# A merged router and expert product, a reordered second phase and a reordered end in a 16-batch transformer kernel

## The reference

```python
x = x + ln(attention(ln(x)))       # 16 heads of 8, softmax over 512 keys
x = x + ln(fp8_ffn(ln(x)))         # 128 x 128 product on values rounded to fp8
x = x + ln(hawk_block(ln(x)))      # below
x = x + ln(moe(ln(x)))             # below

# hawk_block: z = rmsnorm(x) @ W_in; gate, xc = z; xc = causal conv of 4 taps
alpha = exp(-8 * softplus(base) * sigmoid(forget))   # forget, inp = xc @ W_gates
h = linear_recurrence(alpha, sqrt(1 - alpha**2 + 1e-6) * sigmoid(inp) * xc)
x = x + (gelu(gate) * h) @ W_out
x = x + (gelu(xn2 @ W_grow_a) * (xn2 @ W_grow_b)) @ W_shrink   # xn2 = rmsnorm(x)

# moe: 8 experts with one shared weight, capacity 100 tokens for each expert
logits = hs @ w_gate; gate = max(softmax(logits)); best = argmax(logits)
place = running count of the tokens that chose the same expert, over all batches
out = gate * (place < 100) * (hs @ w_expert + b_expert)
```

## Time and profile before

| what | value |
|---|---|
| runs | 1344.32 us median, 1343.93 to 1347.55 |
| the profiled execution | 1344.07 us, of which the span is 1342.4 us |
| PE busy | 1200.6 us (89%) |
| DVE busy | 1117.4 us (83%) |
| ACT busy | 974.6 us (73%) |
| POOL busy | 806.7 us (60%) |
| chain that ended last | PE 36%, DVE 25%, issue 15%, POOL 10%, ACT 10% |

### The profile page before, as it was taken

One profiled execution on the slowest core, in us unless ns is written; L12 is line 12 of the kernel. 1 busy time (PEld: TensorE's weight loads), 2 busy tenths in 40 slices (PEclk: granted clock), 3 DMA queues, 4 the chain that ended last, 5 costly groups with the idle time before them and its releaser, 6 DMA issues.

```text
span 1342.4 us, 26167 instructions
## 1 busy us (share of the span) xinstructions
PE 1200.6 (89%) x8688; PEld 498.3 (37%) x8688; DVE 1117.4 (83%) x2357; ACT 974.6 (73%) x1780; POOL 806.7 (60%) x1091
## 2 busy tenths in 40 slices
PE   1789999999999999999999999988989999999863
PEld 0223233332333333333333332334645555555443
DVE  2877999999999999999999899956668878878756
ACT  1267877888788788878788777787776787787640
POOL 6304447466466566566565545366788888788752
PEclk7589999999999999999999999999999999999985
DMA  1121011011011010110110010000000000000000
GB/s 50 52 89 43 27 45 40 30 43 40 30 44 38 31 43 32 37 44 33 37 45 31 32 37 15 2 1 1 1 9 9 9 17 9 9 16 9 16 9 24
DMA packets 52517, 37.87 MB, mean 28 GB/s; under 512 B 8864, under 2 KB 51744, under 8 KB 52384
## 3 DMA queue, kind: packets, MB, share of 16 engines
q1 hardware_dynamic: 52384, 36.22, 8.4%
HBM read 6.31 MB, written 4.19 MB: 8 GB/s over the span
## 4 chain that ended last, share of the span: by engine, by line
PE 36%; DVE 25%; issue 15%; POOL 10%; ACT 10%; SPq 4%; DMA 0%; ACTq 0%; DVEq 0%; POOLq 0%
PE bank L201 10%; PE bank L182 9%; DVE neg_max L493 9%; PE bank_pair L169 4%; PE bank L228 4%; SPq L644 3%; PE bank L210 3%; ACT probs L381 2%; PE bank L235 2%; DVE probs L1178 2%; PE bank_pair L797 2%; DVE probs L1350 2%; DVE probs L1354 1%; DVE y_q L472 1%; POOL x_all L1497 1%
## 5 line engine op out<-in xcount | busy, mean ns | idle before, releaser
L381 ACT ACTIVATE probs<-bank 128x512 f32<-128x512 f32 x1024 | 569.3, 599 | 166.1 <-PE bank L182 163.8
L493 DVE TENSOR_REDUCE neg_max<-bank_pair 128x2 f32<-128x1024 f32 x512 | 610.3, 1215 | 87.4 <-PE bank_pair L169 85.5
L182 PE MATMUL bank<-q_stack,k_stack 50*128 50x512 bf16 x1024 | 353.1, 388 | 29.9 <-ACT probs L381 22.7
L201 PE MATMUL bank<-probs,v_pad 128*32 128x256 f32 x4096 | 332.2, 394 | 0.4 <-issue 0.2
L169 PE MATMUL bank_pair<-k_stack,q_stack 48*128 48x512 bf16 x1024 | 292.4, 396 | 34.0 <-DMA k_stack<-k_parts 18.1
L182 PEld LDWEIGHTS bank<-q_stack,k_stack 50*128 50x128 bf16 x1024 | 79.7, 94 | 273.8 <-ACT probs L381 233.2
L201 PEld LDWEIGHTS bank<-probs,v_pad 128*32 128x32 f32 x4096 | 83.1, 108 | 167.5 <-issue 160.3
L797 PE MATMUL bank_pair<-probs,w_gates 128*128 128x512 f32 x256 | 118.9, 609 | 1.7 <-issue 1.7
L567 POOL TENSOR_SCALAR tiny<-mv_b 128x4 f32<-128x4 f32 x16 | 3.6, 228 | 147.6 <-DVE mv_b L52 147.6
L522 POOL TENSOR_TENSOR q_rest<-q_rest,q_parts 128x512 f32<-128x512 f32 x16 | 20.2, 1261 | 119.3 <-ACT q_rest L325 119.3
L169 PEld LDWEIGHTS bank_pair<-k_stack,q_stack 48*128 48x128 bf16 x1024 | 54.1, 95 | 59.5 <-DVE neg_max L493 37.3
(11 more groups left out here) (249 smaller groups left out, 2263.6 us busy)
## 6 DMA issues: line engine op xcount, KB each, us to landing
q_stack<-q_parts SPq DMA_DIRECT2D x384, 32.0 KB
k_stack<-k_parts SPq DMA_DIRECT2D x384, 32.0 KB
x_all<-in_z_dram SPq DMA_DIRECT2D x16, 256.0 KB, 3.0
out_dram<-x_all SPq DMA_DIRECT2D x16, 256.0 KB, 2.3
q_stack<-max_rows SPq DMA_DIRECT2D x64, 8.0 KB
w_gates<-in_w_gates_dram SPq DMA_DIRECT2D x1, 512.0 KB, 3.6
w_in<-in_w_in_dram SPq DMA_DIRECT2D x1, 256.0 KB, 2.7
w_grow<-in_w_grow_dram SPq DMA_DIRECT2D x1, 256.0 KB, 3.9
```

The costliest lines, as they stand in the source:

```text
L182: nc.tensor.matmul(st_ps[h][:, :], k_stack[par][rows, p, c * P:(c + 1) * P], q_stack[par][rows, p, :], start=True, stop=True).then_inc(s[" ...
L201: mm = nc.tensor.matmul(acc[32 * g:32 * g + 32, cols], v_pad[bpar][:, kc, 4 * a + g, :], probs[:, at + g, cols], start=(t == 0 and kc == 0 ...
L381: nc.scalar.activation(probs[:, 4 * (n % RING) + g, :], st_ps[g % 2][:, :], ACT.Exp, scale=SCALE)\
L493: nc.vector.tensor_reduce(neg_max[j // 4][:, c, j % 4, :], score_ps[c % 2][:, :, :], AX_X, ALU.max, negate=True).then_inc(s["max_read"], 1)
```

## The change

It does five things, all in the second phase.

1. **Joined product.** The router's weight (128x8) and the expert's (128x128) lie side by side in one tile `w_route_expert` of 136 columns; the logits and the expert product of a chunk come out of one matmul. The result no longer fits one bank, so the last two single banks become a pair: chunks 0 and 1 lie in its first half, chunks 2 and 3 in its second, each 136 columns wide, and the running counts move to column 384 of the second half. `shrink`, which writes the first half, now also waits until the logits have been read (`top_step`).
2. **Order in the loop.** ACT does `decay` ahead of `route_exps`. DVE does `ranks` after `stats_t` instead of ahead of `sum_h`. POOL does `root_x3` ahead of `roots_ahead`.
3. **Order at the start of the drain.** PE does `gate_in` ahead of `cumulated`; ACT does `decay` ahead of `route_exps`.
4. **Order at the end.** POOL: `root_x3(NB+2)` ahead of the routing roots of NB+1. DVE: `norm_x3(NB+2)` ahead of `ranks(NB+2)`; `routed_out(NB+1)` moves from ahead of `raw_x3(NB+2)` to behind `place(NB+2)`. Batch 14 uses the tile `acc_y` and statistics tiles of its own instead of y, so that it needs not wait for y. For the last batch the maximum and the shifted logits come ahead of the sum with the bias, and the statistics' aggregation behind the reciprocal.
5. **Dropped.** The last batch's counts (two small DVE instructions).

```diff
 def routed(i, free=None):                                   # tensor
-                for c in range(C):
-                    mm = nc.tensor.matmul(log_ps[:, c * E:(c + 1) * E], h4T[:, c * P:(c + 1) * P], w["route"][:, :],
-                                          start=True, stop=True)
-                mm.then_inc(s["logits_ps"], 1)
...
                 for c in range(C):
-                    mm = nc.tensor.matmul(bank_y[:, c * D:(c + 1) * D], h4T[:, c * P:(c + 1) * P], w["expert"][:, :],
+                    mm = nc.tensor.matmul(both_ps[:, c // 2, c % 2, :], h4T[:, c * P:(c + 1) * P], w["route_expert"][:, :],
                                           start=True, stop=True)
                 mm.then_inc(s["y_ps"], 1)
-        def shrink(i, free=None):
+        def shrink(i, free=None, after_logits=0):
...
                 if free:
                     wait(pe, *free)
+                    if after_logits:
+                        wait(pe, s["top_step"], 2 * after_logits)
                 else:
                     bank_free(pe, i, live, BANK_Y, "shrink")
+                    if live(i, -4):
+                        wait(pe, s["top_step"], 2 * (i - 3))
...
 PE, drain
             forget(NB)
+            gate_in(NB)
             cumulated(NB)
-            gate_in(NB)
 ACT, loop and drain
+            decay(i)
             route_exps(i)
-            decay(i)
 DVE
+        def y_of(i):
+            return (acc_y, "y_odd") if i == NB + 2 else (y, "y")
+        def largest(i):
+            b, q = i - 4, s["top_step"]
+            wait(dve, s["y_ps"], b + 1)
+            nc.vector.tensor_reduce(top[:, 0, :].rearrange("p (n c) -> p n c", n=2), log_ps, AX_X, ALU.max)\
+                .then_inc(q, 1)
+        def below_largest(i):
...
         def routed(i):
...
+                if i > NB + 2:
+                    largest(i)
+                    below_largest(i)
                 if i > NB + 1:
-                    wait(dve, s["x4_ready"], b)
+                    wait(dve, s["x4_ready"], b - 1)
                 else:
                     wait(dve, s["yc_ready"], b)
...
 DVE, drain
             norm_t(NB + 2)
-            routed_out(NB + 1)
             raw_x3(NB + 2)
             stats_x3(NB + 2)
             routed(NB + 2)
+            norm_x3(NB + 2)
             ranks(NB + 2)
             exps_sum(NB + 2)
             exps_inv(NB + 2)
-            norm_x3(NB + 2)
             counts_of(NB + 2)
             place(NB + 2)
+            routed_out(NB + 1)
             place_sum(NB + 2)
...
-            counts_of(NB + 3)
+            stats_y(NB + 3)
 DVE, loop
             routed(i)
-            ranks(i)
             sum_h(i)
             sum_t(i)
             stats_t(i)
+            ranks(i)
 POOL, loop
             x3_sum(i)
+            root_x3(i)
             roots_ahead(i)
-            root_x3(i)
 POOL, drain
             x3_sum(NB + 2)
+            root_x3(NB + 2)
             routed_root(NB + 1)
             routed_sum(NB + 1)
-            root_x3(NB + 2)
```

More of the change, by code:

```diff
@@ L708, in hawk_moe_phase @@
     xc_pad = padded[:, 0:T + TAPS - 1]
-    stats = {n: (sb(f"bn_{n}", [P, C, 6]), sb(f"mv_{n}", [P, C, 2])) for n in ("t", "x3", "y")}
+    stats = {n: (sb(f"bn_{n}", [P, C, 6]), sb(f"mv_{n}", [P, C, 2])) for n in ("t", "x3", "y", "y_odd")}
     h_sum = sb("h_sum", [P, C])
@@ L909, in cumulated @@
                 for c in range(C - 1):
-                    later = bank_r[:, 2 * C * E + (c + 1) * E:3 * C * E]
+                    later = bank_r[:, CUM + (c + 1) * E:CUM + C * E]
                     nc.tensor.matmul(later, consts["ones"][:, :],
@@ L969, in tensor @@
             routed(NB + 1, (s["t_ready"], NB - 1))
-            shrink(NB + 2, (s["y_ready"], NB - 2))
+            shrink(NB + 2, (s["y_ready"], NB - 2), after_logits=NB - 2)
             cumulated(NB + 1)
@@ L1119, in scalar @@
         if drain:
+            decay(NB)
             route_exps(NB)
-            decay(NB)
             square(NB)
@@ L1191, in taps, with stats_y @@
                     conv[par][:, 1, :], ALU.mult, ALU.add).then_inc(q, 1)
+        def y_of(i):
[6 more added lines that the diff above has]
+        def below_largest(i):
+            b, q = i - 4, s["top_step"]
+            wait(dve, q, 2 * b + 1)
+            wait(dve, s["route_step"], 5 * b)
+            wait(dve, s["exps_ready"], b)
+            TT(by_bank(shifted[:, :, :]), log_ps,
+               by_bank(top[:, 0, :].unsqueeze(2)).to_broadcast([P, 2, 2, E]), ALU.subtract).then_inc(q, 1)
+        def stats_y(i):
+            if live(i, -4):
+                aggregate(y_of(i)[1], "y", i - 4)
         def routed(i):
@@ L1195, in routed @@
                 b = i - 4
+                y, which = y_of(i)
                 wait(dve, s["y_ps"], b + 1)
+                if i > NB + 2:
+                    largest(i)
+                    below_largest(i)
                 if i > NB + 1:
-                    wait(dve, s["x4_ready"], b)
+                    wait(dve, s["x4_ready"], b - 1)
                 else:
                     wait(dve, s["yc_ready"], b)
[L1201 to L1206, removed]
-                wait(dve, s["y_ready"], b + 1)
[L1208 to L1214, removed]
+                TT(y.rearrange("p (n c d) -> p n c d", n=2, c=2), y_ps,
+                   consts["b_expert"][:, :].unsqueeze(1).unsqueeze(1).to_broadcast([P, 2, 2, D]), ALU.add).then_inc(s["y_ready"], 1)
+                if i <= NB + 2:
+                    largest(i)
+                wait(dve, s["y_ready"], b + 1)
+                raw(which, "y", chunk(y))
+                if i <= NB + 2:
+                    below_largest(i)
+                    stats_y(i)
         def routed_out(i):
             b = i - 4
+            y, which = y_of(i)
             wait(dve, s["rs_y_step"], 5 * (b + 1))
-            scaled(y, chunk(y), stats["y"][1], rs["y"][:, 2, :], s["yn_part"])
+            scaled(y, chunk(y), stats[which][1], rs["y"][:, 2, :], s["yn_part"])
             wait(dve, s["yn_part"], C * (i - NB))
@@ L1323, in place_sum @@
                 nc.vector.tensor_reduce(top[:, 6, :], placed[:, :, :], AX_X, ALU.add).then_inc(q, 1)
-                wait(dve, s["count_step"], 2 * b + 1)
-                TT(counts[:, :], counts[:, :], counted[:, :], ALU.add).then_inc(s["count_step"], 1)
+                if b < NB - 1:
+                    wait(dve, s["count_step"], 2 * b + 1)
+                    TT(counts[:, :], counts[:, :], counted[:, :], ALU.add).then_inc(s["count_step"], 1)
                 wait(dve, q, at + 2)
@@ L1699, in build @@
         psum = [ctx.enter_context(nc.psum_tensor(f"bank_pair{i}", [P, 2, T], F32)) for i in range(2)]
-        psum += [ctx.enter_context(nc.psum_tensor(f"bank{i}", [P, T], F32)) for i in range(4)]
+        psum += [ctx.enter_context(nc.psum_tensor(f"bank{i}", [P, T], F32)) for i in range(2)]
+        bank_yr = ctx.enter_context(nc.psum_tensor("bank_pair2", [P, 2, T], F32))
+        psum += [bank_yr[:, 0, :], bank_yr[:, 1, :], bank_yr]
         x_all = sb("x_all", [P, NB, C * D])
```

18 lines of the change are left out of this document (11 added, 7 removed).

## The result

| | before | after |
|---|---|---|
| median of the runs | 1344.32 us | 1336.17 us (1335.66 to 1337.33) |
| the profiled execution | 1344.07 us | 1337.33 us |
| its span | 1342.4 us | 1335.6 us |

Both medians are of four runs; the kernel before ranged from 1343.93 to 1347.55. The ratio is 0.9934, 95% interval 0.9921 to 0.9947: faster by 8 us or 0.66%. The forecast was 1337.5 us. Run once more beside the last experiments, the same kernel gave 1337.48 us (ratio 0.9936, 0.9921 to 0.9952).

The account below looks back on a forecast made before the run. POOL's and DVE's ring of waits, with PE close behind, was taken to bound the loop. The terms 0 - 1.3 - 1.0 + 0.25 - 4.5 = -6.55 from 1344.07 gave 1337.5 us, range 1328 to 1347.

Parts of the forecast that it names:

- G to X: Loop, POOL's `gate_mul` start (G) to `x3_sum` end (X): 13.00 to 12.16 us, since `ranks` leave the way of `sum_h`.
- X to G: Loop, POOL's `x3_sum` end (X) to `gate_mul` start (G): 12.5 us after 11.55, with 3.8 of waits for DVE.
- the signs named: Signs of being right: POOL idle about 1.3 ahead of `root_x3`, three small steps near 1 us each, period within 0.3 of 24.6.
- starved rival: Loop: POOL's L1512 (later L1538) held until the second tap ends; period 25.45, 1344.8 us, or 1349 with PE slowed; chance 0.22.
- Nine batches: The loop's nine batches: period 24.66 against 24.64, so nothing gained; within -2 and +2 for earlier steps.
- the ring: Loop: the repeating cycle of waits between POOL and DVE, 24.55 us a batch, longer than PE's.
- End of the loop against X: DVE's scans end 10.15 behind POOL's `x3_sum` instead of 11.49, so the drain starts earlier: -1.3 us.
- Start of the drain: With `gate_in` ahead PE's product comes 4.8 us earlier; POOL's own queue leaves -1.0 of it; bounds 0 and -4.8.
- Middle: Middle of the drain: `shrink(NB+2)` waits 0.9 longer for the shifted logits, `sum_t` feels +0.25 us; bounds 0 and 0.9.
- End: After `x3_sum(NB+2)`: `routed(NB+3)` starts 4.35 earlier, dropped counts and later aggregation save 0.15; -4.5 us, bounds -3 and -6.
- Joined product: PE: logits and expert product together take 1.03 us, saving 0.75 of PE a batch, counted as nothing in the loop.
- The rival that it doesn't join: 136 columns cost more than two passes of 128: PE 0.2 longer a batch, +2 us on any case; no chance given.

Follow-up runs that it names:

- dve_act_back: The changed kernel with `ranks` ahead of `sum_h` and `route_exps` ahead of `decay` again in the loop, POOL's order staying new; 1336.14 us.
- pool_back: The changed kernel with only POOL's loop order put back, `roots_ahead` ahead of `root_x3`; 1333.57 us.
- gate_back: The changed kernel with PE's `cumulated` ahead of `gate_in` again at the start of the drain; 1339.72 us.
- the split kernel: The changed kernel with each chunk's joined product split into one of 8 and one of 128 columns, same layout; 1337.73 us.
- end_back: The changed kernel with DVE's and POOL's old written order of the end, batch 14's own tile and the short tail kept; 1339.74 us.
- all_loop_back: The changed kernel with all three loop orders (POOL, DVE, ACT) as before; joined product, drain start and end stay new; 1339.67 us.

## Why the prediction was right

**G to X**: forecast 12.16, measured 12.13. The size is right, the reason given isn't needed for it. The 0.84 was put down to `ranks` leaving the way of `sum_h`; dve_act_back has them in the way and loses nothing. The 0.84 is had either way, by the order of `ranks` (pool_back) or by POOL's lateness, which gives DVE the time.

**X to G**: forecast 12.5, measured 12.26. The steps came as described: idle 1.41 (1.4 reckoned), L1538 slipped through in 0.20, L1542 0.56 (0.5 of waiting reckoned), L1544 1.08. L1546 came under the first scan and took 1.92. Over their free times the rows of POOL add up to 3.5 of waits (L1482 0.88, L767 and L768 of `roots_ahead` 0.43, L1542 0.36, L1544 0.85, L1546 0.88, L1550 0.10), where 3.8 was reckoned. Period 24.39 and not 24.66. Of the signs named, the three small steps "each near 1 us" came only in part: 0.56, 1.08 and 1.92, the last being a `pow` of 1.04 with 0.88 of waiting. The starved rival fell on L1538, which was not held. The Trainium skill, "SBUF — State Buffer", section "Who interferes with whom", has the second of two such instructions blocked in full: the trace agrees for L1544 and L1546 (0.85 and 0.88 of waiting). L1538 ran at 1137.00, where one tap of DVE ends (1136.99) and the next begins; it took its free 0.20, and the taps (1.53 for both, 0.75 for one alone) were not held either.

**Nine batches**: 0 forecast, -0.04 measured, and that is luck: two errors cancel, 0.27 less in each equal batch, and 1.6 to 2 lost in the last, when the clock fell. A slip in the reckoning helped: the forecast 24.66 is for a batch of the ring, which took 24.55 before, but it was held against the mean of 24.64, in which three longer batches stand. Like against like, the forecast was +0.11 a batch, 1.0 us in nine, and the whole sum -5.55; the equal batches came out 0.16 shorter. The starved rival had put that loss at some 2.4 us of idle time; it came at 1.64.

**End of the loop against X**: -1.3 forecast. The loop's scans end at 1265.22 instead of 1266.91: -1.7. In the steady batch they end 10.12 behind X instead of 11.48, -1.36, as reckoned.

**Start of the drain**: -1.0 forecast of 4.8. `gh` starts 3.57 earlier (1282.41 against 1285.98), of which 1.7 is the loop's end: -1.9, the double. That POOL, not PE, comes last held (L1504 has no bracket, and is held for 0.9). The path to it did not: `norm_h` was forecast at 15.6 behind the scans, "hardly earlier", and starts 13.06 behind them, where it was 15.83 before. And the 0.8 for a `pow` that no scan holds didn't come: L1506 takes 1.84, as it did before:

```profile
1283.07 1.83 POOL L1480 TENSOR_TENSOR rs_h<-rs_h,pow 128x4 f32<-128x4 f32 x1
```

So 2.8 were gained ahead of `norm_h` and 0.9 lost again in its own wait. What was left out is the clock: behind the transposes `wout` takes 3.75 instead of 3.15 and the grow product 2.55 instead of 1.88. That returns 1.2, so -0.7 is left. PE is idle 7.79 ahead of the transposes, 5.73 before, but this need not be the cause: in gate_back it is 5.73 too, and `wout` takes the same 3.75. gate_back shows that 0.6 of the 1.9 belongs to PE's edit; no run took the other 1.3 apart. ACT's edit at the same place (`decay` ahead of `route_exps`) is the plain candidate and was never undone by itself.

**Middle**: +0.25 forecast, +0.44 measured (from -2.34 at the grow gelu to -1.89 at the last L1523).

**End**: -4.5 forecast, -4.85 measured. DVE was late next, as said: the product at the low clock is done at 1323.6, and L1203 starts at 1325.23, behind two `routed_out`. The product took 2.18 where 2.2 was reckoned.

**Joined product**: 1.03 forecast from start to start, 0.92 measured, nothing in the loop as said; the split kernel shows nothing at the end either, where the forecast had DVE late and not PE. The rival that it doesn't join is ruled out.

The sum forecast was -6.55, the spans differ by -6.8. The measured terms: 0 (nine batches), -1.7, -0.7, +0.44 and -4.85. The end, two thirds of the whole, was forecast by its mechanism; the loop's nothing came by luck, and so did the size of the drain's start, where the larger gain ahead of `norm_h`, the `pow` that was held after all and the fall of the clock nearly offset each other.

## What to carry to other kernels

Two reorderings that each shorten a ring of several engines need not add up: measure the four corners, since one of them can take the idle time from which the other lived. Where an order leaves an engine idle for a result, look for a step that needs no new result and put it there: here the same order cost 0.41 a batch without such a step and saved 0.96 with it. At an end where little overlaps, count each engine's instructions in their written order; that sum came out within 0.4 us.

## What the runs showed of the hardware

- **The same idle time, with and without a slower clock.** Ahead of the last `wout` of the loop PE was idle for 1.64 to 1.68 in five kernels. In three (changed, its repetition, gate_back) that `wout` took 2.84, 2.70 and 2.86 and the batch 26.4; in two (dve_act_back, end_back) it took 2.29 and the batch 24.8. Idle time alone didn't decide it. The 2.44 in gate_back cost next to nothing (3.68 against 3.60); the 2.97 of before cost 1.78. In the drain `wout` took 3.15 and 3.75 behind the same 5.73 (before, gate_back), and 3.08 to 3.75 behind 7.57 to 7.79.
- **Each small POOL instruction under DVE's two-input ones pays for one of them.** L1542, L1544 and L1546 take 0.56, 1.08 and 1.92 in the loop, and 0.20, 0.23 and 1.04 in the drain (from 1318.38), where DVE works on L1181, which has one large input. One that issues where two taps meet (L1538, 0.20) pays nothing.
- **The same order of POOL fell into two patterns of waits.** In all_loop_back the two taps take 1.53, L1376 2.07 and the scans 3.14; in the kernel before, with the same order on POOL, DVE and ACT but the product not joined, the taps take 2.38, L1350 (the later L1376) 1.21 and the scans 3.06. The periods are 24.56 and 24.55.
